# Norm constants of 12 images by a GpSimd power, and image 0 projected to z under the last convolution step

## The chip, the cores and the metric

The kernel runs on one core of one Trainium2 chip. The metric is the device time of one execution in microseconds. The core has five queues that run side by side: TensorE (PE; its weight loads are shown as PEld), VectorE (DVE), ScalarE (ACT), GpSimd (POOL) and SyncE (SP), which issues most DMAs. Each runs its instructions in program order and waits for the others by semaphores.

## The reference, cut to what matters

A residual network over 16 images of 16 x 16 tokens with 192 channels: a group norm and a block-DCT convolution, a gated attention, and a mixture of 8 experts.

```python
x = x + conv(_gn(x), W1, b1)            # 3x3 block DCT, product with W1, gelu, inverse DCT
t = _to_tokens(x)                       # (16, 256, 192)
t = t + attn(_ln_t(t), ...)             # attn normalises its input once more, by ln_w and ln_b
t = t + ffn(_ln_t(t), ...)              # 8 experts, the best 2 for each token

def _ln_t(v, eps=1e-05):
    m = jnp.mean(v, axis=-1, keepdims=True)
    s = jnp.var(v, axis=-1, keepdims=True)
    return (v - m) / jnp.sqrt(s + eps)

# in attn, for each image
normed = _layernorm(x, ln_w, ln_b)      # the second norm
Z = silu(normed @ W_qk.T + b_qk)        # q and k are Z by gamma and beta
q = Z * gamma[0] + beta[0]; k = Z * gamma[1] + beta[1]
A = square(relu(q @ k.T / seq_len))
V = (A @ v) * gate                      # v, gate = silu(normed @ W_hidden.T + b_hidden)
```

Two norms in a row mean two constants for each token: rs1 = 1/sqrt(var + eps), and n_scale, which is 1/sqrt(var * rs1^2 + eps) and is then multiplied by rs1.

## The kernel before

A token tile is 128 partitions; an image has two (HALVES). X lies in SBUF as 128 x 32 tiles x 192. Three stages follow one another, each a software pipeline written out by hand for every engine (`pipeline` calls a step function for i, partly in a hardware loop, and each engine orders the pieces of its step itself): the convolution (CONV, steps -4 to 16), the attention (ATTN, steps -1 to 16) and the experts (MOE).

**Convolution.** In step i VectorE (`conv_step`, L910) adds the convolution of image i-1 into X (L920, from ps_conv), takes that image's moments (L932 to L963) and works out the group norm's constant grs of image i+2 by a bit-trick seed and three Newton rounds (L925 to L977). GpSimd multiplies: xc (L619) and xn (L627). TensorE turns xn into coef of image i+1, multiplies coef of image i by W1 (mix), and transforms the mixed image back (conv, four matmuls into ps_conv, which wait for `conv_read`, the add for image i-1). ScalarE does the squares, the Gelu of mix (L748) and the copy of coef (L751).

**The norm constants.** For the first 12 images (SCALED = 12, 24 columns) VectorE works out rs1 and what follows from it in `first_scales` behind step 12, and n_scale and n_bias in `second_scales` behind step 13. Both use `rsqrt` (L857): the seed, then three rounds of three small instructions, each linked to the one before, that is with a wait for its completion (`Chain.link`). The last four images (8 columns) follow in attention step 0.

**Image 0.** ScalarE's step 15 begins with `normalise(0)` (L697, four activations), which waits for `scales_done`. TensorE's `transpose_normed(0)` stands in step 15 behind mix of image 15. Then, ahead of attention step 0: ScalarE copies the turned image (nB_bias and n_hi, L785, L786), VectorE makes the low parts (L906, L907) ahead of the add for image 15, TensorE projects to z (`z_product(0)`), ScalarE applies Silu (L791) and VectorE makes q and k (`query_key(0)`). `under_conv(i)` is true for image 0. Attention step 0 on TensorE begins with the v products (ten matmuls), then sim, which waits for q and k, then the gates.

**GpSimd.** `set_up_lists`, ten small operations, stands at the start of step 14. In the attention GpSimd does a power for the last norm of each image: u_pow, 128 x 2 (L637), with the exponent from `minus_half`.

All matmuls are issued through a helper at line 1278, so a matmul's line is mostly L1278; the transposes are L1282 and L1283.

Of the kernel before, what the change touches and what calls it, by code (L numbers as in the profile page):

```python
# [195 lines left out]
def build(nc, x, consts, w1, b1, ln_w, ln_b, w_hid, w_qk, b_hid, b_qk, b_i, gamma, beta, w_out, w_out_t, b_out, b_col, w_r,  # L196
# [8 lines left out]
    with ctx:  # L205
# [79 lines left out]
        minus_half = sb("minus_half", [P, HALVES])  # L285
# [129 lines left out]
        scales_done = sem("scales_done")  # L415

# [157 lines left out]
        def _(pool):  # L574
# [8 lines left out]
            chain.link(pool.memset(ln_b_wide, 0.0))  # L583
            pool.wait_ge(ld_const, 16)
# [11 lines left out]
            def set_up_lists():  # L596

                chain.link(pool.memset(pad_rows[:, :], 0.0))
                chain.link(pool.memset(no_offset[:, :], 0))
                chain.link(pool.memset(minus_half[:, :], -0.5))  # L600
                chain.link(pool.memset(next_ids[:, :], HALVES))
                pool.wait_ge(ld_rest, 16)
                chain.link(pool.tensor_copy(pad_rows[:, ID:ID + 1].bitcast(i32), K("pad_id")))
                pool.tensor_copy(list_at[:, :], K("list_base")).then_inc(pads_ready, 1)
                for rows in (row_a, row_b):
                    chain.link(pool.tensor_copy(rows[:, :, ID:ID + 1].bitcast(i32), K("ids").unsqueeze(2)))
                chain.link(pool.tensor_copy(before_bf[:, :], K("before")))
                pool.tensor_copy(ones_bf[:, :], K("ones")).then_inc(bf_set, 1)
                pool.wait_ge(bf_set, 1)

            def conv_step(i, odd):
                if isinstance(i, int) and i == IMAGES - 2:
                    set_up_lists()
                if not absent(i + 3):

                    wait(pool, xn_done, i + 2)
                    wait(pool, sq_done, i + 2)
                    wait_alone(pool, gmean_done, i + 4, ld_const)
                    pool.tensor_tensor(grouped(xc[:, 1 - odd, :, :]), grouped(X[:, tiles(i + 3), :]),  # L619
                                       over_channels(gmean[:, :]), ALU.subtract).then_inc(xc_done, 1)  # L620
                if isinstance(i, int) and i == 0:
                    widen()
                if not absent(i + 2):

                    wait_alone(pool, grs_done, i + 3, ld_const)
                    wait(pool, coef_ps, i + 2)
                    pool.tensor_tensor(grouped(xn[:, :, :]), grouped(xc[:, odd, :, :]),  # L627
                                       over_channels(grs[:, :]), ALU.mult).then_inc(xn_done, 1)
            pipeline(pool, conv_step, **CONV)

            def attn_step(i):
                r = i - 1
                if not absent(r):

                    wait_alone(pool, u_var_done, r + 1, ld_const)
                    wait(pool, u_done, r)
                    pool.tensor_tensor(u_pow[:, :], u_var[:, :], minus_half[:, :], ALU.pow).then_inc(u_pow_done, 1)  # L637
# [55 lines left out]
        def _(act):  # L693
# [13 lines left out]

            def weight_high_parts():
# [26 lines left out]
            def conv_step(i, odd):  # L735
# [4 lines left out]
                if isinstance(i, int) and i == IMAGES - 1:  # L740
                    normalise(0)
                if isinstance(i, int) and i == 1:
                    bias_high_parts()
# [23 lines left out]
            def attn_step(i):  # L767
# [14 lines left out]
                if not absent(i + 1):  # L782

                    act.wait_ge(nT_ps, i + 2)
                    act.activation(nB_bias[0:KB, :], ps_nT[0:KB, 1, :], ACT.Copy).then_inc(nB_bias_done, 1)  # L785
                    act.activation(n_hi[:, :, :], ps_nT, ACT.Copy).then_inc(nT_hi_done, 1)  # L786
# [57 lines left out]
        def _(dve):  # L844
# [12 lines left out]
            def rsqrt(y, v, neg_half_v, work):  # L857


                chain.link(dve.tensor_scalar(y.bitcast(i32), v.bitcast(i32), -0.5, float(0x5F3759DF),  # L860
                                             ALU.mult, ALU.add))
                for n in range(3):
                    chain.link(dve.tensor_tensor(work, neg_half_v, y, ALU.mult))
                    chain.link(dve.tensor_tensor(work, work, y, ALU.mult))
                    last = dve.scalar_tensor_tensor(y, work, 1.5, y, ALU.add, ALU.mult)
                    if n < 2:
                        chain.link(last)
                return last
# [41 lines left out]
            def conv_step(i, odd):  # L910
# [5 lines left out]
                if isinstance(i, int) and i == IMAGES:  # L916
                    low_parts(0)
# [63 lines left out]

            def first_scales(lo, hi):

                mean, var, rs = moments[:, lo:hi, 0], moments[:, lo:hi, 1], rs1[:, lo:hi]
                v, neg, work = ln_var[:, lo:hi], ln_neg[:, lo:hi], ln_work[:, lo:hi]
                dve.tensor_scalar(neg, var, -0.5, -0.5 * LN_EPS, ALU.mult, ALU.add)
                chain.link(dve.tensor_scalar(v, var, LN_EPS, None, ALU.add))
                chain.link(rsqrt(rs, v, neg, work))
# [4 lines left out]

            def second_scales(lo, hi):

                mean, var, rs = moments[:, lo:hi, 0], moments[:, lo:hi, 1], rs1[:, lo:hi]
                v, neg, work = ln_var[:, lo:hi], ln_neg[:, lo:hi], ln_work[:, lo:hi]
                ns, nb = n_scale[:, lo:hi], n_bias[:, lo:hi]
# [3 lines left out]
                dve.tensor_scalar(neg, work, -0.5, -0.5 * LN_EPS, ALU.mult, ALU.add)  # L1002
                chain.link(dve.tensor_scalar(v, work, LN_EPS, None, ALU.add))
                chain.link(dve.tensor_tensor(a_scale[:, lo:hi], a_scale[:, lo:hi], v, ALU.mult))
                chain.link(rsqrt(ns, v, neg, work))
# [4 lines left out]
            def conv_or_scales(i, odd):  # L1010
                conv_step(i, odd)

                if isinstance(i, int) and i == 0:
                    weight_low_parts()
                if isinstance(i, int) and i == 1:
                    bias_low_parts()
                if isinstance(i, int) and i == SCALED:
                    first_scales(0, SCALED * HALVES)
                if isinstance(i, int) and i == SCALED + 1:
                    second_scales(0, SCALED * HALVES)  # L1020
                if isinstance(i, int) and i == SCALED + 2:
                    gate_bias_low()

            pipeline(dve, conv_or_scales, **CONV, chain=chain, per=12)

            def query_key(i):
# [4 lines left out]
                last.then_inc(qk_done, 1)  # L1031

# [143 lines left out]
            def attn_step(i):  # L1176
# [22 lines left out]
                if not absent(i + 1):  # L1199
                    query_key(i + 1)  # L1200
                if isinstance(i, int) and i == 0:
                    first_scales(SCALED * HALVES, IMAGES * HALVES)
                    second_scales(SCALED * HALVES, IMAGES * HALVES)
# [69 lines left out]
        def _(pe):  # L1273
# [52 lines left out]

            def conv_step(i, odd):
                if not absent(i):
# [3 lines left out]
                    pe.wait_ge(coef_done, i + 1)  # L1332
                    for f in range(NFC):
# [21 lines left out]
                if isinstance(i, int) and i == IMAGES - 1:  # L1355
                    transpose_normed(0)
# [23 lines left out]
            def products(dst, hi, lo, columns, n_first, at=slice(0, SEQ)):  # L1380


                wA, wB, wA_lo, wB_lo = hi[:, 0, columns], hi[:, 1, columns], lo[:, 0, columns], lo[0:KBB, 1, columns]
                pairs = ((wA, nA_hi[:, at]), (wA, nA_lo[:, at]), (wB, nB[:, at]), (wB_lo, nB_bias[:, at]),
                         (wA_lo, nA_hi[:, at]))
                for n, (w, x_part) in enumerate(pairs):
                    lhsT, rhs = (x_part, w) if n_first else (w, x_part)
                    last = mm(dst, lhsT, rhs, n == 0, n == len(pairs) - 1)
                return last

            def z_product(i):
                pe.wait_ge(nT_done, i + 1)
                pe.wait_ge(nB_bias_done, i + 1)
                products(ps_z, w_qk_hi, w_qk_lo, slice(0, QK), False).then_inc(z_ps, 1)

# [8 lines left out]
            def attn_step(i):  # L1404
# [12 lines left out]
                if not absent(i):  # L1417
                    gates(0)
# [17 lines left out]
                if not absent(i + 1):  # L1436
                    z_product(i + 1)
# [121 lines left out]
```

## Time and profile before

| | before |
|---|---|
| median of 3 runs | 622.38 us (622.28 to 623.73) |
| the profiled execution, its own time | 623.77 us |
| its span (first to last instruction) | 621.8 us |
| TensorE busy | 576.9 us, 93% |
| VectorE busy | 416.1 us, 67% |
| ScalarE busy | 333.5 us, 54% |
| GpSimd busy | 273.6 us, 44% |
| mean granted TensorE clock | 0.976 of full speed |

All positions are microseconds from the first instruction. Instructions overlap in an engine, so the distance from one start to the next tells more than a duration. The convolution ends on TensorE near 119.3, the attention near 296, and the experts run to the end.

### The profile page before, as it was taken

How to read it: one execution, taken by the hardware profiler on the slowest of the kernel's cores; microseconds unless marked ns; L12 is line 12 of the kernel's file. 1: busy time of each engine (PE TensorE's matmuls, PEld its weight loads, DVE VectorE, ACT ScalarE, POOL GpSimd, SP SyncE). 2: the span in 40 equal slices, each digit the busy share in tenths (PEclk: the TensorE clock that was granted, in tenths of full speed). 3: DMA queues.
4: the chain of work that ended last, by engine and by line, in shares of the span. 5: the costliest groups of instructions: out<-in, count | busy, mean ns of one | idle time of the engine just before them, and what ended most of it. 6: DMA issues, size and time to landing. Idle time of an engine off the chain costs nothing.

```text
span 621.8 us, 14555 instructions
## 1 busy us (share of the span) xinstructions
PE 576.9 (93%) x3844; PEld 542.7 (87%) x3845; DVE 416.1 (67%) x1533; ACT 333.5 (54%) x722; POOL 273.6 (44%) x314
## 2 busy tenths in 40 slices
PE   3999999889999999999189999999999999999993
PEld 2898988777888888888079999999999999999992
DVE  4578888678888888888875555555555555555650
ACT  1433323665666766764365555555555555556650
POOL 3322231214565656656434444444544444445432
PEclk9989999999999999999689999999999999999998
DMA  8970000401111211111232333333333333332221
GB/s 269 407 295 1 0 0 2 172 13 40 48 68 38 70 45 64 51 58 58 77 91 42 49 51 51 51 51 51 51 51 51 51 51 51 44 39 40 40 27 20
DMA packets 31826, 42.41 MB, mean 68 GB/s; under 512 B 4596, under 2 KB 27797, under 8 KB 31670
## 3 DMA queue, kind: packets, MB, share of 16 engines
q0 software_dynamic: 13488, 13.74, 14.1%
q1 hardware_dynamic: 18196, 28.19, 13.7%
q8 instruction: 12, 0.20, 0.1%
q14 instruction: 16, 0.13, 0.1%
q10 hardware_dynamic: 114, 0.15, 0.1%
HBM read 24.49 MB, written 17.57 MB: 68 GB/s over the span
## 4 chain that ended last, share of the span: by engine, by line
PE 38%; DMA 6%; DVE 3%; issue 3%; POOL 1%; POOLq 0%; ACT 0%; DVEq 0%; ACTq 0%
PE ps L1278 36%; DMA out_rows<-const,y_id 6%; PE ps L1282 1%; PE ps L1283 1%; POOL y_id L676 1%; DVE we_lo L1232 0%; POOL out_rows L680 0%; POOLq L205 0%; DVE const L1256 0%; DVE const L1262 0%; DVE over L1095 0%; DVE n_tiles L1097 0%; ACT we_hi L820 0%; DVE table_parts L1100 0%; DVE table_parts L1105 0%
## 5 line engine op out<-in xcount | busy, mean ns | idle before, releaser
L829 ACT ACTIVATE hT<-ps,b_i_sb 128x256 f32<-128x256 f32 (+1 forms) x240 | 95.2, 447 | 118.9 <-PE ps L1278 118.9
L1278 PE MATMUL ps<-w_o_sb,hT 128*128 x852 | 145.2, 326 | 0.9 <-DVE const L1256 0.9
L680 POOL DMA_INDIRECT out_rows<-const,y_id x71 | 125.8, 1772 | 42.0 <-POOL y_id L676 29.4
L1278 PEld LDWEIGHTS ps<-w_o_sb,hT 128*128 128x128 f32 x852 | 137.5, 190 | 1.2 <-issue 1.2
L1278 PE MATMUL ps<-n_hi,we_hi 128*128 128x256 f32 (+1 forms) x480 | 129.1, 291 | 4.2 <-DVE n_hi L1240 2.5
L1278 PEld LDWEIGHTS ps<-n_hi,we_hi 128*128 128x128 f32 x480 | 92.1, 192 | 5.0 <-DVE we_lo L1232 4.8
L1278 PE MATMUL ps<-n_hi,we_lo 128*128 128x256 f32 (+1 forms) x480 | 96.1, 282 | 0.0
L1232 DVE TENSOR_TENSOR we_lo<-we_all,we_hi 128x768 fp32r<-128x768 f32 x80 | 73.2, 956 | 22.3 <-issue 21.1
L1278 PEld LDWEIGHTS ps<-n_hi,we_lo 128*128 128x128 f32 x480 | 74.3, 192 | 0.0
L1278 PE MATMUL ps<-nA_lo,we_hi 128*128 128x256 f32 (+1 forms) x240 | 67.7, 282 | 0.0
L1256 DVE TENSOR_TENSOR const<-ps,b_o_sb 128x384 f32<-128x384 f32 (+1 forms) x40 | 20.5, 512 | 69.9 <-PE ps L1278 38.9
L820 ACT ACTIVATE we_hi<-we_all 128x768 fp32r x80 | 63.5, 848 | 1.2
L676 POOL TENSOR_TENSOR y_id<-y_row,no_offset 128x2 int32<-128x2 int32 (+1 forms) x40 | 8.8, 220 | 123.6 <-DVE const L1262 105.9
L1278 PE MATMUL ps<-attnT,hT 128*128 128x256 f32 x192 | 44.2, 380 | 2.3 <-issue 2.3
L1278 PEld LDWEIGHTS ps<-nA_lo,we_hi 128*128 128x128 f32 x240 | 45.9, 191 | 0.0
L1238 DVE TENSOR_TENSOR nA_lo<-ps,n_hi 128x256 fp32r<-128x256 f32 (+1 forms) x40 | 15.8, 394 | 41.9 <-ACT n_hi L836 41.9
L627 POOL TENSOR_TENSOR xn<-xc,grs 128x384 f32<-128x384 f32 x16 | 13.9, 867 | 64.6 <-DVE grs L977 54.1
L660 POOL DMA_INDIRECT lists<-row_a,slots x32 | 32.9, 1027 | 20.9 <-DVE row_b L1081 12.0
L1278 PEld LDWEIGHTS ps<-attnT,hT 128*128 128x128 f32 x192 | 35.2, 190 | 6.6 <-issue 2.5
L1278 PE MATMUL ps<-conv_only,coef 96*108 96x192 f32 x192 | 38.9, 356 | 0.4
L1278 PE MATMUL ps<-w_out_sb,hT 128*128 128x200 f32 x192 | 36.7, 341 | 1.1 <-DVE hT L1194 1.0
L1278 PEld LDWEIGHTS ps<-w_out_sb,hT 128*128 128x128 f32 x192 | 31.8, 190 | 4.5 <-DVE hT L1194 2.9
(235 smaller groups left out, 1166.8 us busy)
## 6 DMA issues: line engine op xcount, KB each, us to landing
we_all<-in_w_i SPq DMA_DIRECT2D x8, 768.0 KB, 13.3
conv_only<-lists SPq DMA_DIRECT2D x31, 194.0 KB, 2.8
w_o_sb<-in_w_o SPq DMA_DIRECT2D x8, 576.0 KB, 18.1
out_rows<-X SPq DMA_DIRECT2D x16, 192.0 KB
X<-in_x SPq DMA_DIRECT2D x1, 1536.0 KB, 10.9
out_rows<-const,y_id POOLq DMA_INDIRECT x71, 3.6
conv_only<-lists SPq DMA_DIRECT2D x9, 97.0 KB, 2.3
we_all<-in_w_hid SPq DMA_DIRECT2D x1, 776.0 KB, 7.3
```

Of the source, the lines that this page charges most:

```text
L627: pool.tensor_tensor(grouped(xn[:, :, :]), grouped(xc[:, odd, :, :]), over_channels(grs[:, :]), ALU.mult).then_inc(xn_done, 1)
L660: pool.indirect_dma_start(out=lists, out_offset=bass.IndirectOffsetOnAxis(ap=slots[:, c, t:t + 1], axis=0), in_=rows[:, t, :], in_offset=N ...
L676: pool.tensor_tensor(y_id[:, odd, 0:n], y_row[:, odd, 0:n], no_offset[:, 0:n], ALU.add).then_inc(id_done[odd], 1)
L680: pool.indirect_dma_start(out=out, out_offset=bass.IndirectOffsetOnAxis(ap=y_id[:, odd, t:t + 1], axis=0), in_=y_sb[:, odd, t, :], in_offs ...
L820: act.activation(we_hi[:, 1 - odd, here].unsqueeze(1), we_all[:, ds(e, 1), here], ACT.Copy).then_inc(we_hi_done, 1)
L829: last = act.activation(hT[:, odd, f, 0:n].unsqueeze(1), ps_h[:, b, c, 0:n].unsqueeze(1), ACT.Gelu, bias=b_i_sb[:, ds(e * FCHUNKS + f, 1)])
L1232: last = dve.tensor_tensor(we_lo[:, 1 - odd, here].unsqueeze(1), we_all[:, ds(e, 1), here], we_hi[:, 1 - odd, here].bitcast(f32).unsqueeze ...
L1238: dve.tensor_tensor(sA_lo[:, 0:n * P], ps_sT[:, 0, 0:n * P], sA_hi[:, 0:n * P].bitcast(f32), ALU.subtract)
L1256: dve.tensor_tensor(here, ps_y[:, 0:n, :], b_o_sb[:, ds(e, 1), :].broadcast_to((P, n, D)), ALU.add).then_inc(y_read, 1)
L1278: return pe.matmul(dst, lhsT, rhs, start=start, stop=stop)
L1282: pe.transpose(dst[:, 0, here], rows[:, 0:KA], K("ident"))
L1283: return pe.transpose(dst[:, 1, here], rows[:, KA:WIDE], K("ident"))
```

## The change

The reciprocal roots of the first 12 images' variances are no longer worked out by VectorE alone. Behind step 12 VectorE writes the variance and signals (`first_variance`, `ln_var_done`). GpSimd raises it to -0.5 at the end of its own step 12, one instruction on 128 x 24. Behind step 13 VectorE waits for it (`ln_pow_done`), does one Newton round (`refine`), then the rest of `first_scales`, then the second variance. GpSimd raises that at the end of its step 13, and behind step 14 VectorE refines it and does the rest of `second_scales`. The four late images keep the seed and three rounds.

Image 0: ScalarE's `normalise(0)` is followed in step 15 by the copies of the turned image (`high_parts`), ahead of the Gelu of image 15. On TensorE the transposes of image 0 stand ahead of mix of image 15, and `z_product(0)` behind it, ahead of the transform back of image 15. VectorE's `low_parts(0)` stands at the end of step 15, and `query_key(0)` at the start of step 16, ahead of the add for image 15. The gates of image 0 on TensorE wait for that add (`conv_read`).

```diff
@@ GpSimd
             chain.link(pool.memset(ln_b_wide, 0.0))
+            chain.link(pool.memset(minus_half[:, :], -0.5))
...
-                chain.link(pool.memset(minus_half[:, :], -0.5))
...
+                for n, rs in enumerate((rs1, n_scale)):
+                    if isinstance(i, int) and i == SCALED + n:
+                        early = slice(0, SCALED * HALVES)
+                        pool.wait_ge(ln_var_done, n + 1)
+                        pool.tensor_tensor(rs[:, early], ln_var[:, early], minus_half[:, :],
+                                           ALU.pow).then_inc(ln_pow_done, 1)
             pipeline(pool, conv_step, **CONV)
@@ ScalarE
                 if isinstance(i, int) and i == IMAGES - 1:
                     normalise(0)
+                    high_parts(0)
@@ VectorE
-                if isinstance(i, int) and i == IMAGES:
-                    low_parts(0)
...
+            def refine(rs, lo, hi):
+                y, neg, work = rs[:, lo:hi], ln_neg[:, lo:hi], ln_work[:, lo:hi]
+                chain.link(dve.tensor_tensor(work, neg, y, ALU.mult))
+                chain.link(dve.tensor_tensor(work, work, y, ALU.mult))
+                chain.link(dve.scalar_tensor_tensor(y, work, 1.5, y, ALU.add, ALU.mult))
...
+            def conv_or_scales(i, odd):
+                if isinstance(i, int) and i == IMAGES:
+                    dve.wait_ge(ld_attn, 16 * 5)
+                    query_key(0)
+                conv_step(i, odd)
...
+                early = (0, SCALED * HALVES)
+                if isinstance(i, int) and i == SCALED:
+                    first_variance(*early).then_inc(ln_var_done, 1)
+                if isinstance(i, int) and i == SCALED + 1:
+                    dve.wait_ge(ln_pow_done, 1)
+                    refine(rs1, *early)
+                    first_scales(*early)
+                    second_variance(*early).then_inc(ln_var_done, 1)
+                if isinstance(i, int) and i == SCALED + 2:
+                    dve.wait_ge(ln_pow_done, 2)
+                    refine(n_scale, *early)
+                    second_scales(*early)
+                    gate_bias_low()
+                if isinstance(i, int) and i == IMAGES - 1:
+                    low_parts(0)
@@ TensorE
                     pe.wait_ge(coef_done, i + 1)
+                    if isinstance(i, int) and i == IMAGES - 1:
+                        transpose_normed(0)
...
                 if isinstance(i, int) and i == IMAGES - 1:
-                    transpose_normed(0)
+                    z_product(0)
...
                 if not absent(i):
+                    if under_conv(i):
+                        pe.wait_ge(conv_read, IMAGES)
                     gates(0)
```

## Rows read from the trace of the kernel before

**Rows 1.** Windows: stretch, length, busy per engine (instructions), granted clock, DMA share, GB/s.

```profile
105.00:110.00 5.00, 5.00 (x36) 4.92 (x35) 4.46 (x24) 1.36 (x2) 1.30 (x4) 1.00 0.00 2
110.00:115.00 5.00, 3.53 (x25) 3.29 (x24) 4.34 (x20) 3.00 (x6) 1.45 (x7) 1.00 0.18 59
```

**Rows 2.** Timeline of TensorE: start, length, engine, line, operation, count, wait before it.

```profile
102.08 1.57 PE L1278 MATMUL ps<-conv_only,const 108*128 108x192 f32 x8
...
110.41 1.63 PE L1278 MATMUL ps<-const,xn 128*96 128x216 f32 x12
113.52 1.54 PE L1278 MATMUL ps<-conv_only,const 108*128 108x192 f32 x8 [1.47 <-DVE X L920]
114.89 2.12 PE L1278 MATMUL ps<-conv_only,coef 96*108 96x192 f32 x12
...
117.18 0.27 PE L1283 MATMUL ps<-const,normed 128*128 128x128 f32 x1
117.76 1.57 PE L1278 MATMUL ps<-conv_only,const 108*128 108x192 f32 x8 [0.30 <-ACT conv_only L748]
119.70 0.28 PE L1278 MATMUL ps<-n_hi,w_qk_hi 128*32 128x256 f32 x1 [0.38 <-DVE n_hi L907]
...
120.29 0.34 PE L1278 MATMUL ps<-w_hi,n_hi 128*128 128x392 f32 x1
```

**Rows 3.** Timeline of VectorE, the same columns, end of step 12 to end of step 14.

```profile
100.89 0.17 DVE L986 TENSOR_SCALAR ln_neg<-moments 128x24 f32<-128x24 f32 x1
...
102.03 0.18 DVE L863 TENSOR_TENSOR ln_work<-ln_neg,rs 128x24 f32<-128x24 f32 x1
...
103.77 0.18 DVE L865 SCALAR_TENSOR_TENSOR rs<-ln_work,rs 128x24 f32<-128x24 f32 x1
...
104.61 0.55 DVE L920 TENSOR_TENSOR X<-X,ps 128x384 f32<-128x384 f32 x1
...
108.22 0.19 DVE L977 SCALAR_TENSOR_TENSOR grs<-newton,grs 128x32 f32<-128x32 f32 x1
...
108.76 0.93 DVE L1002 TENSOR_SCALAR ln_neg<-ln_work 128x24 f32<-128x24 f32 x1
...
112.73 0.18 DVE L1008 SCALAR_TENSOR_TENSOR n_bias<-moments,n_scale 128x24 f32<-128x24 f32 x1
112.83 0.55 DVE L920 TENSOR_TENSOR X<-X,ps 128x384 f32<-128x384 f32 x1
...
114.45 0.17 DVE L963 COPY moments<-mom 128x4 f32<-128x4 f32 x1
```

**Rows 4.** Timeline of ScalarE: coef of image 15, normalise(0), Gelu of image 15.

```profile
112.08 0.71 ACT L751 ACTIVATE coef<-ps 96x648 f32<-96x648 f32 x1 [0.82 <-PE ps L1278]
112.94 1.65 ACT L704 ACTIVATE normed<-X,n_bias,n_scale 128x192 f32<-128x192 f32 x4 [0.15 <-DVE n_bias L1008]
117.05 0.65 ACT L748 ACTIVATE conv_only<-ps 108x576 f32<-108x576 f32 x1 [2.46 <-PE ps L1278]
```

**Rows 5.** Timeline of GpSimd: xn of images 14 and 15, the last power.

```profile
101.11 0.86 POOL L627 TENSOR_TENSOR xn<-xc,grs 128x384 f32<-128x384 f32 x1 [3.34 <-DVE grs L977]
108.55 0.90 POOL L627 TENSOR_TENSOR xn<-xc,grs 128x384 f32<-128x384 f32 x1 [6.58 <-DVE grs L977]
...
303.60 0.82 POOL L637 TENSOR_TENSOR u_pow<-u_var,minus_half 128x2 f32<-128x2 f32 x1
```

**Rows 6.** Groups of GpSimd by line: operation, count, busy us, mean ns, idle before.

```profile
L637 POOL TENSOR_TENSOR u_pow<-u_var,minus_half 128x2 f32<-128x2 f32 x16 | 11.8, 738 | 14.1 <-DVE u_var L1140 13.8
L649 POOL TENSOR_TENSOR row_a<-row_a,next_ids 128x2 int32<-128x2 int32 x16 | 3.0, 188 | 1.1 <-DMA lists<-row_b,slots 1.1
```

**Rows 7.** Windows where attention turns into experts (PE, PEld, DVE, ACT, POOL, clock).

```profile
298.00:300.00 2.00, 0.17 (x2) 0.09 (x3) 1.76 (x12) 0.00 (x0) 1.06 (x1) 0.64 0.00 0
...
312.00:314.00 2.00, 2.00 (x12) 2.00 (x11) 1.79 (x11) 0.15 (x1) 1.70 (x2) 0.50 0.46 151
```

**Rows 8.** Timeline of VectorE under that last power.

```profile
303.87 0.29 DVE L1042 TENSOR_TENSOR above<-above,equal 128x128 f32<-128x128 f32 x1
```

More of the change, by code:

```diff
@@ L284, in build @@
         u_pow = sb("u_pow", [P, HALVES])
-        minus_half = sb("minus_half", [P, HALVES])
+        minus_half = sb("minus_half", [P, SCALED * HALVES])
         next_ids = sb("next_ids", [P, HALVES], i32)
@@ L415, in build @@
         scales_done = sem("scales_done")
+        ln_var_done, ln_pow_done = sem("ln_var_done"), sem("ln_pow_done")
         normed_done, nT_ps, nT_done, z_ps, z_done, qk_done = (
@@ L636, in attn_step @@
                     wait(pool, u_done, r)
-                    pool.tensor_tensor(u_pow[:, :], u_var[:, :], minus_half[:, :], ALU.pow).then_inc(u_pow_done, 1)
+                    pool.tensor_tensor(u_pow[:, :], u_var[:, :], minus_half[:, 0:HALVES], ALU.pow).then_inc(u_pow_done, 1)
                 if not absent(i):
@@ L706, in normalise, with high_parts @@
                 last.then_inc(normed_done, 1)
+            def high_parts(i):
+                act.wait_ge(nT_ps, i + 1)
+                act.activation(nB_bias[0:KB, :], ps_nT[0:KB, 1, :], ACT.Copy).then_inc(nB_bias_done, 1)
+                act.activation(n_hi[:, :, :], ps_nT, ACT.Copy).then_inc(nT_hi_done, 1)
             def weight_high_parts():
@@ L781, in attn_step @@
                     act.activation(gateT[:, :, :], ps_gate, ACT.Silu).then_inc(gate_done, 1)
[L782 to L786, printed above, removed]
+                if not absent(i + 1) and not under_conv(i + 1):
+                    high_parts(i + 1)
                 if not absent(i + 1) and not (isinstance(i, int) and i < 0):
@@ L855, in token_moments, with seed @@
                 chain.link(last)
[L857 to L868, printed above, removed]
+            def seed(rs, lo, hi):
+                chain.link(dve.tensor_scalar(rs[:, lo:hi].bitcast(i32), ln_var[:, lo:hi].bitcast(i32), -0.5,
+                                             float(0x5F3759DF), ALU.mult, ALU.add))
             def weight_low_parts():
@@ L980, in conv_step, with first_variance @@
                     chain.wait()
+            def first_variance(lo, hi):
+                var, v, neg = moments[:, lo:hi, 1], ln_var[:, lo:hi], ln_neg[:, lo:hi]
+                dve.tensor_scalar(neg, var, -0.5, -0.5 * LN_EPS, ALU.mult, ALU.add)
+                return dve.tensor_scalar(v, var, LN_EPS, None, ALU.add)
             def first_scales(lo, hi):
[L984 to L988, printed above, removed]
+                mean, rs, v = moments[:, lo:hi, 0], rs1[:, lo:hi], ln_var[:, lo:hi]
                 chain.mark(dve.tensor_scalar(r_scale[:, lo:hi], rs, 1.0, None, ALU.add))
@@ L992, in first_scales, with second_variance, second_scales @@
                 dve.scalar_tensor_tensor(r_bias[:, lo:hi], mean, -1.0, rs, ALU.mult, ALU.mult)
[L994 to L998, printed above, removed]
+            def second_variance(lo, hi):
+                var, rs, work = moments[:, lo:hi, 1], rs1[:, lo:hi], ln_work[:, lo:hi]
                 chain.link(dve.tensor_tensor(work, var, rs, ALU.mult))
                 chain.link(dve.tensor_tensor(work, work, rs, ALU.mult))
-                dve.tensor_scalar(neg, work, -0.5, -0.5 * LN_EPS, ALU.mult, ALU.add)
-                chain.link(dve.tensor_scalar(v, work, LN_EPS, None, ALU.add))
+                dve.tensor_scalar(ln_neg[:, lo:hi], work, -0.5, -0.5 * LN_EPS, ALU.mult, ALU.add)
+                return dve.tensor_scalar(ln_var[:, lo:hi], work, LN_EPS, None, ALU.add)
+            def second_scales(lo, hi):
+                mean, rs, v = moments[:, lo:hi, 0], rs1[:, lo:hi], ln_var[:, lo:hi]
+                ns, nb = n_scale[:, lo:hi], n_bias[:, lo:hi]
                 chain.link(dve.tensor_tensor(a_scale[:, lo:hi], a_scale[:, lo:hi], v, ALU.mult))
-                chain.link(rsqrt(ns, v, neg, work))
                 chain.link(dve.tensor_tensor(a_scale[:, lo:hi], a_scale[:, lo:hi], ns, ALU.mult))
@@ L1008, in second_scales @@
                 dve.scalar_tensor_tensor(nb, mean, -1.0, ns, ALU.mult, ALU.mult).then_inc(scales_done, 1)
[L1010 to L1024, printed above, removed]
+            def refine(rs, lo, hi):
[3 more added lines that the diff above has]
+                chain.link(dve.scalar_tensor_tensor(y, work, 1.5, y, ALU.add, ALU.mult))
             def query_key(i):
@@ L1031, in query_key @@
                 last.then_inc(qk_done, 1)
+            def conv_or_scales(i, odd):
[3 more added lines that the diff above has]
+                conv_step(i, odd)
+                if isinstance(i, int) and i == 0:
+                    weight_low_parts()
+                if isinstance(i, int) and i == 1:
+                    bias_low_parts()
+                early = (0, SCALED * HALVES)
[13 more added lines that the diff above has]
+                    low_parts(0)
+            pipeline(dve, conv_or_scales, **CONV, chain=chain, per=12)
             def choose(r):
@@ L1198, in attn_step @@
                     scale_tokens(r)
-                if not absent(i + 1):
+                if not absent(i + 1) and not under_conv(i + 1):
                     query_key(i + 1)
                 if isinstance(i, int) and i == 0:
-                    first_scales(SCALED * HALVES, IMAGES * HALVES)
-                    second_scales(SCALED * HALVES, IMAGES * HALVES)
+                    late_images = (SCALED * HALVES, IMAGES * HALVES)
+                    for rs, variance, scales in ((rs1, first_variance, first_scales),
+                                                 (n_scale, second_variance, second_scales)):
+                        chain.link(variance(*late_images))
+                        seed(rs, *late_images)
+                        for n in range(3):
+                            refine(rs, *late_images)
+                        scales(*late_images)
                 if isinstance(i, int) and i == IMAGES - 1:
@@ L1325, in prepare, with products, z_product @@
                 last.then_inc(prep_ps, 1)
+            def products(dst, hi, lo, columns, n_first, at=slice(0, SEQ)):
+                wA, wB, wA_lo, wB_lo = hi[:, 0, columns], hi[:, 1, columns], lo[:, 0, columns], lo[0:KBB, 1, columns]
+                pairs = ((wA, nA_hi[:, at]), (wA, nA_lo[:, at]), (wB, nB[:, at]), (wB_lo, nB_bias[:, at]),
+                         (wA_lo, nA_hi[:, at]))
+                for n, (w, x_part) in enumerate(pairs):
+                    lhsT, rhs = (x_part, w) if n_first else (w, x_part)
+                    last = mm(dst, lhsT, rhs, n == 0, n == len(pairs) - 1)
+                return last
+            def z_product(i):
+                pe.wait_ge(nT_done, i + 1)
+                pe.wait_ge(nB_bias_done, i + 1)
+                products(ps_z, w_qk_hi, w_qk_lo, slice(0, QK), False).then_inc(z_ps, 1)
             def conv_step(i, odd):
@@ L1378, in _ @@
             pe.wait_ge(prep_done, 2)
[L1380 to L1394, printed above, removed]
             def gates(c):
@@ L1435, in attn_step @@
                     mm(ps_rows_all, ones_bf[:, :], in_row[:, :]).then_inc(prefix_ps, 1)
-                if not absent(i + 1):
+                if not absent(i + 1) and not under_conv(i + 1):
                     z_product(i + 1)
```

## Prediction

> **What bounds the kernel now.** The page's slices come first: TensorE is busy in nine tenths or more of nearly every slice, so the change can pay only where TensorE has a gap or where its work starts earlier. The table of windows around the end of the convolution shows the place [rows 1]: TensorE is full from 105 to 110 us and has 3.53 us of work in the 5 us after that, while VectorE is busy 4.34 there. TensorE's timeline names the gap [rows 2]: the transform back of image 14 starts at 113.52 after 1.47 us of waiting for VectorE's add into X (L920). VectorE's timeline says why it was late [rows 3]: behind the conv part of step 12 it runs the whole of first_scales (100.89 to 104.61), behind that of step 13 the whole of second_scales (108.33 to 112.83), and only then the add for image 13 at 112.83. A chain link on 128x24 takes 0.217 us: 8 links from 102.03 to 103.77. So the end of the convolution is set by VectorE's small linked instructions. ScalarE's timeline has the other consumer [rows 4]: normalise(0) starts at 112.94, right behind n_bias (112.73).
>
> The mark by which I measure is the first v product of the attention on TensorE, at 120.29 [rows 2]. From there on, no queue changes its order except image 0's own z and q/k steps, which are then done, and the four late images keep the same instructions on VectorE. So a shift of that mark is a shift of the end, microsecond for microsecond.
>
> **The change part by part, with the pow at no cost first.** In what follows T is the time of one 128x24 pow on GpSimd.
>
> Removed from VectorE: two seeds and two of the three Newton rounds of both constants, 2 x 7 links = 3.0 us. Moved: first_scales goes from the end of step 12 to the end of step 13, second_scales from 13 to 14, so that the conv parts of steps 13 and 14 now come ahead of them.
>
> Step 13. After step 12 only two variance instructions remain, so the add for image 12 waits for its matmuls alone: they end at 102.08 + 1.57 = 103.65 [rows 2], a wake-up of 0.15 (the matmul at 113.52 starts 0.14 after the add at 112.83 + 0.55 ends) gives 103.80 instead of 104.61, which is 0.8 us earlier. The conv part takes what it took, 104.61 to 108.33 (grs at 108.22, and 0.11): it ends at 107.52. Then come refine (3 links, 0.65), first_scales (2 links, two unlinked at 0.1: 0.63) and second_variance (2 links, one at 0.1, the last: 0.62 until the next instruction starts), 1.90 together. In these falls the multiplication xn of image 15 on GpSimd, which started 0.33 behind grs and lasted 0.90 [rows 5]. Before, it held the instruction at 108.76 for 0.93 us against 0.18 elsewhere, so I add 0.75 here too. The add for image 13 starts at 110.2, well before 112.83, and TensorE meets no wait there: coef of image 15 at 110.41, the transform back of image 14 at about 111.9 instead of 113.52, ready for step 15 at 113.3.
>
> Step 14. The conv part takes 112.83 to 114.62 (the copy at 114.45 and 0.17), 1.8 us: to 112.0. Refine and second_scales are 6 links and a last instruction, 1.3 + 0.18, and I add 0.2 because GpSimd's nine small set-up operations now run beside them. Scales are done at 113.7, against 112.91 before. So although 3.0 us of links are gone, scales come 0.8 us later: 1.8 us of conv part were put ahead of them, the added wait for TensorE's matmuls gives back only 0.8, and the held instruction stays.
>
> Step 15. normalise(0) takes 1.65 us [rows 4]: 113.75 to 115.4 (ScalarE's own coef ends at 112.79, so it doesn't hold it). TensorE now has the four transposes of image 0 ahead of mix of image 15, and waits for normed: from 113.3 to 115.45. The 1.47 us gap has moved and grown to 2.1. What is queued behind that wait is everything: mix of image 15, for which ScalarE's Gelu waits, then conv(15). The transposes cost 0.44 (mix ended at 114.89 + 2.12 = 117.01, the last transpose at 117.18 + 0.27), mix starts at 115.9, Gelu 2.16 later as before (114.89 to 117.05), the transform back 0.71 later (117.05 to 117.76): 118.77. The next matmul follows 1.37 behind (113.52 to 114.89): v at 120.15 instead of 120.29.
>
> Image 0's copies on ScalarE, its low parts on VectorE and z on TensorE lie beside mix and Gelu. From the last transpose's end (117.45) to z it took 2.25 us before (119.70), with Gelu in between. The same from 116.3 gives z at 118.55, its 0.59 us end at 119.15, and conv(15) would come 0.4 later than 118.77. Without Gelu ahead of the copies the z should just fit under Gelu, so I take 0, and keep 0.4 as the cost if that cover fails. query_key(0) ahead of the add for image 15 on VectorE delays that add, and the gates on TensorE wait for it, but they come behind ten v products and sim, so nothing waits. The memset of minus_half at the start stands where GpSimd waits for data: 0. The store of pads and the late expert loads start within about 2 us of where they did and are needed in the expert stage: 0.
>
> So with the pow free the mark moves by -0.15 us.
>
> **The pow.** The trace has it only on 128x2, at 0.738 us mean, against 0.188 for an integer add of the same shape on the same engine [rows 6]. How the extra 0.55 splits into a part paid once and a part paid per column is not shown. If all is paid once, T = 0.74. If all is per column, T = 0.19 + 24 x 0.275 = 6.8. The first pow starts at 102.0, behind xn of image 14 (101.11 + 0.86) [rows 5], and is wanted at 107.5: free up to 5.5. The second starts at 110.35, behind the variance, and is wanted at 112.0: free up to 1.55 with its wake-up, from there one for one. Between ends so far apart I take the geometric middle, 2.2: the nearest row is the same operation, but 12 times as many columns can't be wholly free. That costs 0.65 us on the second pow.
>
> Sum: -0.15 + 0.65 = +0.5 us. The profiled execution took 623.77 with a span of 621.8, so 1.97 lies outside the span; its changed twin would have a span of 622.3 and a time of 624.25. The median of the runs, 622.38, is 1.39 below the profiled one: 622.85.
>
> **Rivals.** (a) Slower: the pow runs column by column, at or near T = 6.8. Place: the wait for the second pow in step 14. The first ends at 108.8, 1.3 after it is wanted. With xn behind it the variance is out at 111.4, the second pow ends at 118.2, scales at 119.85, normed at 121.55, and the mark is 4.75 later, at 126.3: +6.0. TensorE would then idle from 113.3 to 121.6. At the end of the attention, in the two stretches of [rows 7], the granted clock fell to 0.64 on average while TensorE did 0.17 us of work in 2 us, and at 312 to 314, with TensorE fully busy again, it still was 0.50, 1.2 of 2.4 GHz. About 4 us of work at that level costs 2 us: 630.4 in all. It decides from T = 1.55, and passes 0.3% from T = 3.6. For it: 0.55 us is a lot for two columns of setup alone. Against it: nothing shows that the columns are not overlapped.
> The Trainium skill, GPSIMD Engine Reference, section "Performance versus the Vector engine", says that the engine's tensor_tensor is a software loop over elements; by that rule this rival is the natural one, and the trace agrees for plain arithmetic, where 128x384 took 0.87 and 128x2 0.19.
> A second question on this rival is whether a pow holds VectorE as xn does. Under the pow at 303.60 VectorE's 128x128 operation with two SBUF inputs at 303.87 took 0.29 [rows 5, 8], where xn kept the held one for 0.93, so I say no.
> The same page (section "Key points") says that GpSimd's SBUF interfaces are shared with VectorE and contend with instructions of two SBUF inputs; the trace agrees for xn and not for the pow. By the rule a pow of 6.8 us would also hold step 13 from 104.6 to 108.8 and this rival would be some 3 us worse; by the row it is as above; the forecast with T = 2.2 is the same by both.
>
> (b) Better than forecast: T is below 1.55 and the stalls that I added (0.75, 0.2) don't come. Scales are then done at 112.75, normalise starts behind coef at 112.8, normed 114.45, the mark at 119.2: -1.1, 621.3. This is a floor for the chain as written. More than that would need TensorE not to wait for normed at all (mark at about 117.95, -2.3, 620.0), which VectorE's order excludes.
>
> (c) The change doesn't do what it says: TensorE's gap goes in step 14 and comes back whole in step 15, T is small and the z cover fails by 0.4: 622.6. It lies inside the forecast.
>
> **From these to the numbers.** Forecast and (c), T up to 3.6: 0.60, own range 622.2 to 624.2. (a): 0.32, from 624.2 up to 630.4, evenly, so some 0.11 beyond 628. (b): 0.08, of which half beyond what I can account for. About 0.3% (1.9 us) is what a measurement of this kernel tells from no change. Faster by that: 0.04; within: 0.63; slower: 0.33. The range 621.2 to 628.2 leaves out 0.04 below and about 0.11 above.
>
> **What would show it.** Right: VectorE's add for image 13 near 110.2 and no wait of TensorE for it; a new TensorE wait of about 2 us for normed ahead of mix of image 15; scales done at 113.7 or later, the more so the longer the pow; the first v product within 0.6 us of 120.3. Wrong: a pow on 128x24 of 4 us or more (rival a, with a clock of 0.5 behind it), a wait of VectorE for the first pow, or a first v product before 119.2. Should the mark move and the end not move with it, my claim on the stages behind it is what failed.

## The result, and the profile after

The changed kernel is slower, by about 0.7%. Nine runs have a median of 630.06 us (625.55 to 630.65), the kernel before 622.47 over nine beside them (621.96 to 626.86). The ratio of the two sets of runs is 1.0071, with a 95% interval from 1.0045 to 1.0096, which is 626.9 us on that median and inside my range. The median itself is 1.9 us above the range: the nine times lie in two groups, 625.6 to 626.0 (three, mean granted clock 0.973 to 0.975) and 629.6 to 630.7 (six, 0.968 to 0.969), and a median falls into one of them. The means differ by 5.2 us. I had given "within 0.3%" 0.63 and "slower" 0.33. What happened is rival (a) at a middling price.

The profiled execution took 629.6 us with a span of 627.7. GpSimd's timeline shows the two powers (start, length, line, operation), answering to [rows 5, 6]:

```profile
100.89 4.21 POOL L634 TENSOR_TENSOR rs<-ln_var,minus_half 128x24 f32<-128x24 f32 x1
106.99 0.85 POOL L628 TENSOR_TENSOR xn<-xc,grs 128x384 f32<-128x384 f32 x1 [1.90 <-DVE grs L978]
109.09 4.17 POOL L634 TENSOR_TENSOR n_scale<-ln_var,minus_half 128x24 f32<-128x24 f32 x1 [1.24 <-DVE ln_var L1003]
```

A power on 128x24 takes 4.2 us, not the 2.2 that I took. VectorE's timeline, answering to [rows 3]:

```profile
103.81 0.17 DVE L936 TENSOR_TENSOR newton<-gneg,grs 128x32 f32<-128x32 f32 x1
...
106.39 0.18 DVE L1017 TENSOR_TENSOR ln_work<-ln_neg,rs 128x24 f32<-128x24 f32 x1
...
107.03 0.85 DVE L992 TENSOR_SCALAR r_scale<-rs 128x24 f32<-128x24 f32 x1
...
108.92 0.55 DVE L921 TENSOR_TENSOR X<-X,ps 128x384 f32<-128x384 f32 x1
...
110.54 0.17 DVE L964 COPY moments<-mom 128x4 f32<-128x4 f32 x1
113.36 0.18 DVE L1017 TENSOR_TENSOR ln_work<-ln_neg,n_scale 128x24 f32<-128x24 f32 x1 [2.65 <-POOL n_scale L634]
...
114.66 0.18 DVE L1012 SCALAR_TENSOR_TENSOR n_bias<-moments,n_scale 128x24 f32<-128x24 f32 x1
```

The first power is free: refine follows grs at 106.39 with no wait, and the first power had ended at 105.1. One instruction is held by xn (0.85 at 107.03). The second power is awaited for 2.65 us. TensorE's timeline, answering to [rows 2]:

```profile
101.05 1.57 PE L1307 MATMUL ps<-conv_only,const 108*128 108x192 f32 x8
...
110.85 1.48 PE L1307 MATMUL ps<-conv_only,const 108*128 108x192 f32 x8
116.67 0.45 PE L1311 MATMUL ps<-const,normed 128*128 128x128 f32 x1 [4.34 <-ACT normed L711]
...
117.55 3.95 PE L1307 MATMUL ps<-conv_only,coef 96*108 96x192 f32 x12
...
122.24 1.57 PE L1307 MATMUL ps<-conv_only,const 108*128 108x192 f32 x8
123.51 0.48 PE L1307 MATMUL ps<-w_hi,n_hi 128*128 128x392 f32 x1
```

The old wait of 1.47 us ahead of the transform of image 14 is gone, and a wait of 4.34 us for normed has come ahead of the transposes. Mix then takes 3.95 us for what took 2.12. The windows say why (busy of PE, PEld, DVE, ACT, POOL, then the granted clock):

```profile
110.00:114.00 4.00, 2.33 (x17) 1.99 (x15) 1.15 (x7) 0.93 (x2) 3.82 (x5) 1.00 0.00 0
114.00:118.00 4.00, 1.33 (x6) 1.35 (x7) 2.88 (x11) 1.86 (x5) 1.16 (x6) 0.55 0.53 114
118.00:122.00 4.00, 4.00 (x17) 3.51 (x15) 0.85 (x2) 1.12 (x3) 0.00 (x0) 0.59 0.93 338
```

TensorE stopped at 112.3, and the clock fell from 2.4 to 1.2 GHz near 114. In steps of half a microsecond the fall lies at 114.4, 2.1 us after TensorE's last matmul, and the return at 121.3, 4.6 us after matmuls resumed; in the kernel before, it had stayed at 1.00 here [rows 1].

Executions do not reach this place at the same time, so I measure a **distance**: from the start of the transform back of image 12 to the first v product. Before it is 120.29 - 102.08 = 18.21 us [rows 2], after 123.51 - 101.05 = 22.46: 4.25 us more.

### The profile page after: what moved, and what is told of

The parts are those of the page before. It is cut to its first block, busy times and chain, and to the rows that moved or that the text cites. A ratio compares the mean times of both kernels' runs of the same rounds, so it can differ in the third digit from the quotient of the medians.

```text
span 627.7 us, 14545 instructions
## 1 busy us (share of the span) xinstructions
PE 579.5 (92%) x3844; PEld 545.2 (87%) x3845; DVE 413.8 (66%) x1519; ACT 335.3 (53%) x722; POOL 280.6 (45%) x316
## 4 chain that ended last, share of the span: by engine, by line
PE 38%; DMA 6%; DVE 3%; issue 3%; POOL 1%; POOLq 0%; ACT 0%; DVEq 0%; ACTq 0%
PE ps L1307 36%; DMA out_rows<-const,y_id 6%; PE ps L1311 1%; PE ps L1312 1%; POOL y_id L683 1%; POOL out_rows L687 0%; DVE we_lo L1261 0%; POOLq L205 0%; DVE const L1285 0%; DVE over L1118 0%; DVE const L1291 0%; DVE n_tiles L1120 0%; ACT we_hi L831 0%; DVE table_parts L1123 0%; DVE table_parts L1128 0%
## 5 line engine op out<-in xcount | busy, mean ns | idle before, releaser
L1307 PE MATMUL ps<-w_o_sb,hT 128*128 x852 | 145.2, 326 | 0.9 <-DVE const L1285 0.9
L687 POOL DMA_INDIRECT out_rows<-const,y_id x71 | 123.3, 1737 | 42.0 <-POOL y_id L683 29.4
L1307 PE MATMUL ps<-attnT,hT 128*128 128x256 f32 x192 | 45.6, 389 | 2.3 <-issue 2.3
```

The costliest lines, as they stand in the source:

```text
L687: pool.indirect_dma_start(out=out, out_offset=bass.IndirectOffsetOnAxis(ap=y_id[:, odd, t:t + 1], axis=0), in_=y_sb[:, odd, t, :], in_offs ...
L1307: return pe.matmul(dst, lhsT, rhs, start=start, stop=stop)
```

## The experiments

The theory (A): the second power is late, the order of image 0 puts mix of image 15 behind it, and the idle TensorE loses its clock. The main rival (B): the new order of image 0 costs by itself.

**A short operation in place of the powers.** It leaves out the reciprocal root for 12 images (a constant stands for it) and keeps every wait and order.

```diff
-                        pool.tensor_tensor(rs[:, early], ln_var[:, early], minus_half[:, :],
-                                           ALU.pow).then_inc(ln_pow_done, 1)
+                        pool.tensor_tensor(rs[:, early], minus_half[:, :], minus_half[:, :],
+                                           ALU.add).then_inc(ln_pow_done, 1)
```

> GpSimd's two 128x24 powers are replaced by a 128x24 addition of two constants (-1 in place of the reciprocal root, so the norms of 12 images are wrong; every queue keeps its order and its waits). The distance from the transform back of image 12 to the first v product on TensorE was 18.21 us before and 22.46 after. Theory A (the second power is late by its 4.2 us, and TensorE's clock falls while it waits): with about 0.25 us for the operation the distance is 17.9 (my own chain of the prediction gives 18.06), TensorE's clock stays at full speed there, time 622 +- 0.7. Rival B (the new order of image 0 alone loses the time, by the wait for normed ahead of mix of image 15): the distance stays above 20, time above 624.

TensorE's timeline, the marks and the wait:

```profile
99.75 1.57 PE L1307 MATMUL ps<-conv_only,const 108*128 108x192 f32 x8
...
112.90 0.30 PE L1311 MATMUL ps<-const,normed 128*128 128x128 f32 x1 [1.87 <-ACT normed L711]
...
117.50 0.48 PE L1307 MATMUL ps<-w_hi,n_hi 128*128 128x392 f32 x1
```

Distance 17.75, clock at 1.00 there, a wait of 1.87 us for normed (I had put 2.1 in the prediction). The ratio is 1.0009 (0.9969 to 1.0049), median 624.24. Without the power's length the change is worth 0.46 us at the mark, the first v product. B falls.

**Each part alone.** First the constants by the powers, with image 0 in the old order (the edit undoes the moves of image 0 that the diff shows: transposes behind mix, copies, low parts, z, q and k behind the convolution).

```diff
...
                 if isinstance(i, int) and i == IMAGES - 1:
-                    z_product(0)
+                    transpose_normed(0)
...
```

> The powers stay, image 0's steps stand in the order of the kernel before (transposes behind mix of image 15, copies, low parts, z, q and k behind the convolution). Theory A with both parts needed (late power times the order that puts everything behind it): mix of image 15 runs under the power, normed is as late as after, distance about 18.8, one short idle of about 2.3 us and no fall of the clock: time about 623. If the late power alone makes the whole loss: distance above 21, time above 626. Rival B: distance 18.2 or less.

Then image 0 in the new order, with the constants from VectorE alone, behind steps 12 and 13 as before.

```diff
...
+                def whole(rs, variance, scales):
+                    early = (0, SCALED * HALVES)
+                    chain.link(variance(*early))
+                    seed(rs, *early)
+                    for n in range(3):
+                        refine(rs, *early)
+                    scales(*early)
                 if isinstance(i, int) and i == SCALED:
...
+                    whole(rs1, first_variance, first_scales)
                 if isinstance(i, int) and i == SCALED + 1:
...
+                    whole(n_scale, second_variance, second_scales)
...
```

> The constants are worked out on VectorE alone at the places of the kernel before (seed and three rounds behind steps 12 and 13), image 0 in the new order. Theory A: normed is ready as before, the transposes wait for nothing that matters, z lies under the Gelu: distance about 17.5, time 621.7. Rival B: the transposes ahead of mix cost by themselves: distance above 19, time above 623.5.

TensorE's timelines, of the constants alone:

```profile
100.90 1.57 PE L1303 MATMUL ps<-conv_only,const 108*128 108x192 f32 x8
...
112.01 2.12 PE L1303 MATMUL ps<-conv_only,coef 96*108 96x192 f32 x12
116.42 0.33 PE L1307 MATMUL ps<-const,normed 128*128 128x128 f32 x1 [2.28 <-ACT normed L711]
...
119.82 0.34 PE L1303 MATMUL ps<-w_hi,n_hi 128*128 128x392 f32 x1
```

and of image 0 alone:

```profile
99.68 1.57 PE L1301 MATMUL ps<-conv_only,const 108*128 108x192 f32 x8
...
111.10 1.54 PE L1301 MATMUL ps<-conv_only,const 108*128 108x192 f32 x8 [1.46 <-DVE X L915]
...
115.59 0.30 PE L1301 MATMUL ps<-n_hi,w_qk_hi 128*32 128x256 f32 x1 [0.55 <-DVE n_hi L904]
...
116.20 1.46 PE L1301 MATMUL ps<-conv_only,const 108*128 108x192 f32 x8
117.37 0.48 PE L1301 MATMUL ps<-w_hi,n_hi 128*128 128x392 f32 x1
```

Distances 18.92 (+0.71 on the kernel before) and 17.69 (-0.52): the parts sum to +0.2, together they make +4.25. The powers alone make normed as late as in the changed kernel (transposes 15.52 behind the transform of image 12, against 15.62), but mix runs meanwhile, the idle time is 2.28 us and the clock stays at 1.00. Image 0's order alone helps. The ratios, 1.0027 (0.9989 to 1.0066) and 1.0006 (0.9962 to 1.0050), can't tell either from no change, so these readings rest on the distance alone, in one profile each; the one kernel that was profiled twice, below, gave the same distance both times. The times that I expected were missed in all three runs so far: the medians of 624.24, 625.95 and 623.02 us lie 1.3 to 3.0 us above them, and the kernel before had 623.63 beside them.

**A filler for the clock.** Matmuls that nobody reads, ahead of the transposes, where TensorE idled. They change nothing that normed waits for. The first run has 21 of them, the second 11, with the same edit but for the number.

```diff
                     if isinstance(i, int) and i == IMAGES - 1:
+                        for _ in range(21):
+                            mm(ps[:, 6, 0:2 * FCH], K("ones"), K("fwd0"))
                         transpose_normed(0)
```

> The kernel after, with 21 matmuls whose result nobody reads put on TensorE ahead of the transposes of image 0 (128x216, about 0.19 us each, 4 us in all), where it idled 4.3 us. Theory A, its clock part: TensorE's clock stays at full speed through the convolution's end, the transposes start where they did (normed is not changed), and the distance falls from 22.46 to about 20.3; time lower than after by 2 us or more. If the clock did not matter: the distance stays 22.4 or grows with the filler.

> The filler again, but 11 matmuls: in the run with 21 each took 0.37 us and not 0.19, so the filler outlasted the wait for normed by 3 us. 11 take about 4.1 us and end before normed is ready (15.5 us behind the transform back of image 12, in both runs). Theory A: clock at full speed there, the transposes as soon as normed is ready, distance from the transform back of image 12 to the first v product 20.1, against 22.46 after. If the clock's fall was no cost: 22.4.

TensorE's timeline with 21:

```profile
102.92 1.57 PE L1307 MATMUL ps<-conv_only,const 108*128 108x192 f32 x8
...
121.70 0.27 PE L1311 MATMUL ps<-const,normed 128*128 128x128 f32 x1
...
126.28 0.48 PE L1307 MATMUL ps<-w_hi,n_hi 128*128 128x392 f32 x1
```

With 21 the filler was too long, 0.37 us each: it outlasted normed, and the distance was 126.28 - 102.92 = 23.36, ratio 1.0100 (1.0067 to 1.0134). What I had wrong was the price of a filler matmul: the clock stayed at 1.00, and from the transposes to v it took 4.58 us, against 6.84 in the changed kernel. With 11, TensorE's timeline:

```profile
103.49 1.57 PE L1307 MATMUL ps<-conv_only,const 108*128 108x192 f32 x8
...
119.24 0.33 PE L1311 MATMUL ps<-const,normed 128*128 128x128 f32 x1 [0.45 <-ACT normed L711]
...
119.73 2.12 PE L1307 MATMUL ps<-conv_only,coef 96*108 96x192 f32 x12
...
123.86 0.48 PE L1307 MATMUL ps<-w_hi,n_hi 128*128 128x392 f32 x1
```

The distance is 20.37 (I expected 20.1). The transposes start 15.75 behind the transform of image 12, as late as after (15.62). But the clock is 1.00, mix takes 2.12, and from the transposes to v it is 4.62 us instead of 6.84. The fall of the clock costs 2.2 us of the 4.25. The one execution took 629.5 us; the section on the prediction says what else was in it.

**The second power twice.**

```diff
                         pool.wait_ge(ln_var_done, n + 1)
+                        if n:
+                            chain.link(pool.tensor_tensor(rs[:, early], ln_var[:, early], minus_half[:, :], ALU.pow))
```

> The kernel after with the second power done twice, one after the other. Theory A: everything from the scales on is later by a whole power and its link, 4.2 to 4.4 us, TensorE idles 8.7 us ahead of the transposes, the clock falls as it did: distance 26.7 to 27.5, time 630 to 635. If something else than the wait for the second power set the loss: distance below 25.

VectorE's wait, and TensorE's:

```profile
123.13 0.18 DVE L1019 TENSOR_TENSOR ln_work<-ln_neg,n_scale 128x24 f32<-128x24 f32 x1 [6.89 <-POOL n_scale L636]
```

```profile
106.57 1.57 PE L1309 MATMUL ps<-conv_only,const 108*128 108x192 f32 x8
...
126.44 0.45 PE L1313 MATMUL ps<-const,normed 128*128 128x128 f32 x1 [8.59 <-ACT normed L713]
...
132.88 0.47 PE L1309 MATMUL ps<-w_hi,n_hi 128*128 128x392 f32 x1
```

Both waits grow by 4.24 and 4.25 us, one for one with the added power. Distance 26.31, 0.4 less than I expected: the clock was back 3.8 us after the matmuls resumed, not 4.6. The time was 637.09 in one run, 2 us above the range that I expected; 13.7 us of low clock near the start stand in its profile.

**The second power cut in two.** Images 0 and 1 first (4 columns); the other 20 columns are refined at the end of VectorE's step 15, and ScalarE waits for them ahead of image 2.

```diff
...
+                for n, rs, lo, hi in ((0, rs1, 0, SCALED * HALVES), (1, n_scale, 0, FIRST),
+                                      (1, n_scale, FIRST, SCALED * HALVES)):
...
+                    refine(n_scale, 0, FIRST)
+                    second_scales(0, FIRST)
...
+                    dve.wait_ge(ln_pow_done, 3)
+                    refine(n_scale, FIRST, SCALED * HALVES)
+                    second_scales(FIRST, SCALED * HALVES)
...
```

> The kernel after with the second power cut in two: columns 0 to 3 first (images 0 and 1), then columns 4 to 23, whose Newton round and scales come at the end of VectorE's step 15. If a power costs a fixed part and a part per column (128x2 0.74, 128x24 4.19: 0.42 and 0.157 a column), it takes 1.05 us on 4 columns and 3.56 on 20. Theory A: the 4 columns are ready before VectorE asks, no wait, distance 17.75 as in the run with the short operation, no fall of the clock there, time 621.9. If each power took some 4 us whatever its width: distance 22.4 or more.

The groups of GpSimd in this kernel, by shape:

```profile
L635 POOL TENSOR_TENSOR rs<-ln_var,minus_half 128x24 f32<-128x24 f32 x1 | 4.2, 4205 | 0.0
L635 POOL TENSOR_TENSOR n_scale<-ln_var,minus_half 128x20 f32<-128x20 f32 x1 | 3.5, 3531 | 0.0
L635 POOL TENSOR_TENSOR n_scale<-ln_var,minus_half 128x4 f32<-128x4 f32 x1 | 1.0, 1012 | 1.2 <-DVE ln_var L1004 1.2
```

TensorE's marks and the wait:

```profile
106.39 1.57 PE L1311 MATMUL ps<-conv_only,const 108*128 108x192 f32 x8
...
119.26 0.30 PE L1315 MATMUL ps<-const,normed 128*128 128x128 f32 x1 [1.59 <-ACT normed L712]
...
123.86 0.48 PE L1311 MATMUL ps<-w_hi,n_hi 128*128 128x392 f32 x1
```

Four widths lie close to one line: (3.531 - 1.012) / 16 = 0.157 us a column and 0.38 us once; 24 columns give 4.16 (measured 4.17 and 4.21), 2 give 0.70 (0.74 in [rows 6]). Distance 123.86 - 106.39 = 17.47, no fall of the clock there: 5.0 us under the changed kernel's 22.46. Median 623.26, ratio 1.0004 (0.9975 to 1.0034).

**The same, with image 0 in the old order**, so that mix runs while normed is made. The edit is both edits together, the cut of the second power and the return to the old order; the part on TensorE in step 15 is shown. It ran twice.

```diff
...
-                    z_product(0)
+                    transpose_normed(0)
...
```

> The second power cut in two as in the run before it, and image 0 in the order of the kernel before (mix of image 15 ahead of the transposes). Theory A with the order as the second factor: mix runs while VectorE and ScalarE make normed (ready about 13.1 us behind the transform back of image 12), nothing waits long, z and v follow the low parts: distance about 16.4, time about 620.6, the best of all. If the new order of image 0 is worth its 0.5 us here too: distance 17.75 or more.

> The same kernel as the split power with image 0 in the old order, once more, because its interval (0.9947 to 1.0011) held no change. Theory A: distance from the transform back of image 12 to the first v product 16.6 again, 1.6 us under the kernel before, ratio about 0.9975. If the ratio lies at 1.000 or above in this run too, the 1.6 us are lost again in later stages.

TensorE's timeline in the first of them:

```profile
103.39 1.57 PE L1308 MATMUL ps<-conv_only,const 108*128 108x192 f32 x8
...
114.50 2.12 PE L1308 MATMUL ps<-conv_only,coef 96*108 96x192 f32 x12
116.46 0.28 PE L1312 MATMUL ps<-const,normed 128*128 128x128 f32 x1
...
120.03 0.34 PE L1308 MATMUL ps<-w_hi,n_hi 128*128 128x392 f32 x1
```

The transposes follow mix with no wait at all. Distance 16.64 in both, 1.57 us under the kernel before. So what the new order of image 0 is worth depends on when normed is ready: alone it gave 0.52 us, here it costs 0.83 (17.47 against 16.64). With the split power the new order waits 1.59 us for normed ahead of mix; the old order runs mix in that time. The ratios are 0.9979 (0.9947 to 1.0011) and 0.9986 (0.9959 to 1.0013), medians 621.69 and 623.66 against 623.44 and 623.81. It is the shortest way to the mark. Over the whole it is better than the changed kernel, whose interval against the kernel before starts at 1.0045; that it beats the kernel before is not shown.

## Why the prediction was right in its range and wrong in its sum, step by step

**The failed step is the size of T.** The range held the ratio because rival (a) stood in it, at 0.32; the sum, +0.5 us, fell short of the ratio's 4.4. I put the power on 128x24 at 2.2 us, the geometric middle between 0.74 and 6.8; it is 4.2, the first of the signs that I had named for being wrong. The mechanism was the one that I priced for rival (a): the wait for the second power in step 14, one for one from T = 1.55. By the prediction's own chain, 4.17 costs -0.15 + 2.62 = +2.5, and the fall of the clock 2 more: 4.5 us. The mark moved by 4.25. In pieces from the runs: -0.46 without the power's length (the short operation), +2.47 by the wait (transposes at 15.62 instead of 13.15 behind the transform of image 12), +2.24 by the clock (6.84 instead of 4.60 from the transposes to v).

**Right.** The add for image 13 was early and TensorE's wait for it went. A new wait for normed came ahead of the transposes, and scales came late although 14 links are gone: 0.5 us later than before, measured from the transform of image 12, even with the short operation. The parts put ahead of them outweigh the links. The first power was free. xn held one VectorE instruction for 0.85 us, as I carried over, while nothing was held under the powers. z lay under the Gelu in the changed kernel and with the short operation: the transform back of image 15 started 0.71 us behind the Gelu, as in the kernel before.

**Right in kind, small in size.** With the power free I expected -0.15 at the mark; the short operation gave -0.46. The add for image 13 came 0.25 us earlier than my 110.2, put on the same scale, and of the 0.2 us for the set-up operations beside the scales 0.1 came there, and nothing in the changed kernel. The cost of 0.4 us that I kept in case z's cover failed did come in one run, with image 0's order alone: there z waited for its low parts (0.55 us at 115.59), and the transform back started 1.13 us behind the Gelu instead of 0.71.

**Wrong beside it.** I had the clock fall only in the worst case of rival (a), with 8 us of idle time. It fell 2.1 us into a wait of 4.3 us here, so a T of 4 cost more than its wait. And the mark does not carry to the end microsecond for microsecond in each execution. From the mark to the last instruction it took 501.5 us before and 504.2 after. The changed kernel's profile has two more stretches at 1.2 GHz, 141.7 to 145.2 and 326.1 to 329.5, where the attention and the experts start up; the kernel before ran at full clock in both places. But the nine other profiles, of kernels that are nearly alike behind the mark, have 501.9 to 504.0 us there, with one such stretch or another or none. So I hold the 2.7 us for where the falls happened to lie in this execution, not for the change; that is argued from these profiles, not tried. The changed kernel was profiled once, in the longer group of its runs.

The same at the start explains why the total tells so little. The transform back of image 12 began between 98.56 us (clock low from 26.5 to 30.0) and 106.57 us (low from 27.8 to 41.5) in the eleven profiles, whose code up to there is nearly the same. The 629.5 us of the run with 11 filler matmuls had 10.2 us of low clock at the start and 3.4 more at 325.

## What to carry to other kernels

Before an operation is widened, measure it at two widths: one row can't tell a price per call from a price per column, and a factor of nine (0.74 to 6.8 us) hung on that. Ask of every wait what stands behind it in the queue: the same late power cost 0.7 us at the mark with mix ahead of the wait and 4.25 with mix behind it, 2.2 of them by the clock. Where a few microseconds are at stake under a clock that moves, measure the distance between two marks in the profile beside the total.

## What the hardware did that I had not expected

GpSimd's power costs 0.38 us and 0.157 us per column (widths 2, 4, 20 and 24), some 70 times a column of a plain product (0.90 us for 384 in [rows 5]). VectorE ran beside it unhindered: under the second power its copy at 110.54 took 0.17 us, and under the first none of its instructions took longer than in the kernel before. The clearest pair is one product of the Newton rounds with two SBUF inputs. Under the first power it took 0.17 us (at 103.81 in the changed kernel); under a plain GpSimd operation (xc) it took 0.69, in the kernel before:

```profile
79.93 0.86 POOL L619 TENSOR_TENSOR xc<-X,gmean 128x384 f32<-128x384 f32 x1 [0.27 <-POOL xn L627]
80.15 0.69 DVE L935 TENSOR_TENSOR newton<-gneg,grs 128x32 f32<-128x32 f32 x1
```

The Trainium skill, GPSIMD Engine Reference, section "Performance versus the Vector engine", has the engine loop over elements in software, and the four widths agree with that. The Trainium skill, GPSIMD Engine Reference, section "Key points", says that GpSimd's SBUF interfaces are shared with VectorE and contend with its instructions in a 2-port mode or with two SBUF inputs. The trace agrees for xc above, not for the powers. The instructions that xn held (0.93 us at 108.76 before, 0.85 at 107.03 after) have one SBUF input, so they are not the case of two inputs that the prediction took them for; no run here shows in which mode they ran.

TensorE's clock fell from 2.4 to 1.2 GHz 2.1 us after its last matmul in the changed kernel and in the one with two powers, and did not fall in idle times of 2.28 us (constants alone) and 1.87 us (short operation). The 2.28 us without a fall are longer than the 2.1 us, so these rows give no length of a wait that is safe. It came back 3.8 to 4.6 us after work resumed. 4.2 us of useless matmuls in the gap kept it up.
